# A two-stage attention kernel on one Trainium2 core: the exponentials of the window scores and the row maxima's copy, rest and parts are placed one step later in the written-out order of the steps

## What is computed

```
scores = einsum(q, k) / sqrt(16)
scores = exp(scores - max(scores))        # first exponential, row maximum over all 1024 keys
scores = where(-32 <= j - i <= 31, scores, 0)
weights = softmax(scores)                 # second exponential
x1 = layernorm(x + (weights @ v) @ Wo)
```

## Time and profile before

| what | value |
|---|---|
| median of 3 executions | 2041.89 us (2038.99 to 2049.73) |
| profiled execution, its own time | 2045.43 us |
| its span in the profile | 2043.6 us |
| TensorE busy | 1794.1 us (88%) |
| VectorE busy | 1602.4 us (78%) |
| ScalarE busy | 1342.1 us (66%) |
| GpSimd busy | 898.5 us (44%) |
| mean granted TensorE clock | 0.96 |

### The profile page before, as it was taken

One profiled execution on the slowest core, in us unless ns is written; L12 is line 12 of the kernel. 1 busy time (PEld: TensorE's weight loads), 2 busy tenths in 40 slices (PEclk: granted clock), 3 DMA queues, 4 the chain that ended last, 5 costly groups with the idle time before them and its releaser, 6 DMA issues. The chain is left out here.

```text
span 2043.6 us, 49487 instructions
## 1 busy us (share of the span) xinstructions
PE 1794.1 (88%) x16304; PEld 1334.9 (65%) x16304; DVE 1602.4 (78%) x4371; ACT 1342.1 (66%) x2643; POOL 898.5 (44%) x1338
## 2 busy tenths in 40 slices
PE   3989999999999999999999636878888699999997
PEld 2546556565565565565655526777787589999997
DVE  2788998988979979989889536978886477777775
ACT  2798898888888878888888315757664244344342
POOL 4323433566555645655565552000303755555411
PEclk8999999999999999999999658999998899999999
DMA  6443536446455464465354629888874333333211
GB/s 215 125 121 97 159 110 176 132 125 178 150 135 158 128 192 123 145 188 159 108 151 121 166 95 299 260 251 307 273 229 151 107 89 96 91 96 96 83 39 39
DMA packets 207317, 304.84 MB, mean 149 GB/s; under 512 B 48429, under 2 KB 108890, under 8 KB 207066
## 3 DMA queue, kind: packets, MB, share of 16 engines
q1 hardware_dynamic: 157322, 195.73, 32.7%
q0 software_dynamic: 29440, 68.98, 11.9%
q10 hardware_dynamic: 20304, 36.97, 4.9%
HBM read 104.16 MB, written 115.87 MB: 108 GB/s over the span
## 5 line engine op out<-in xcount | busy, mean ns | idle before, releaser
L1487 DVE CUSTOM_DVE_ANT_0 above<-p_half,above 128x512 f32<-128x512 f32 x1024 | 680.3, 684 | 102.0 <-ACT above L1171 79.7
L1171 ACT ACTIVATE above<-p_diff 128x512 f32<-128x512 f32 x1024 | 593.7, 600 | 88.8 <-PE p_diff L1047 85.7
L1047 PE MATMUL p_diff<-d_stack,q_stack 96*128 96x512 bf16 x1024 | 392.8, 386 | 30.2 <-ACT above L1171 15.7
L1051 PE MATMUL p_half<-k_stack,q_stack 96*128 96x512 bf16 x1024 | 388.7, 382 | 22.0 <-DVE row_max L1487 20.9
L1809 POOL DMA_INDIRECT raw<-sorted_y,slot x192 | 202.8, 1056 | 348.7 <-DMA sorted_y<-y_tile 293.6
L222 POOL DMA_INDIRECT sorted_x<-y,slot x192 | 198.6, 1035 | 95.9 <-issue 48.9
L2056 ACT ACTIVATE pt_hi<-p_one 128x512 fp32r<-128x512 f32 x128 | 69.5, 595 | 246.2 <-PE p_one L1932 246.2
L1192 ACT ACTIVATE w_win<-p_win 128x512 f32<-128x512 f32 x256 | 153.9, 601 | 50.1 <-PE p_win L1072 45.2
L1047 PEld LDWEIGHTS p_diff<-d_stack,q_stack 96*128 96x128 bf16 x1024 | 98.6, 98 | 110.9 <-ACT above L1171 49.3
L1051 PEld LDWEIGHTS p_half<-k_stack,q_stack 96*128 96x128 bf16 x1024 | 100.5, 99 | 96.6 <-DVE row_max L1487 78.3
L1200 ACT ACTIVATE w_win<-w_win 128x512 f32<-128x512 f32 x256 | 163.3, 638 | 0.2
(11 more groups left out here) (277 smaller groups left out, 4824.6 us busy)
## 6 DMA issues: line engine op xcount, KB each, us to landing
sorted_x<-zeros SPq DMA_DIRECT2D x141, 256.0 KB, 3.0
x_tile<-sorted_x SPq DMA_DIRECT2D x141, 256.0 KB, 4.1
sorted_y<-y_tile ACTq DMA_DIRECT2D x141, 256.0 KB, 3.6
q_stack<-q_parts SPq DMA_DIRECT2D x256, 96.0 KB, 2.4
k_stack<-k_parts SPq DMA_DIRECT2D x256, 96.0 KB, 2.4
d_stack<-d_parts SPq DMA_DIRECT2D x256, 48.0 KB, 2.0
v_win<-v_tiles POOLq DMA_DIRECT2D x16, 544.0 KB, 6.0
v_win<-v_tiles POOLq DMA_DIRECT2D x32, 272.0 KB, 6.8
```

The lines of the kernel that those rows point to most:

```text
L1047: nc.tensor.matmul(p_diff[s % 2][:], qs, d_stack[0:SPLIT_ROWS, h, :], start=True, stop=True).then_inc(s_diff, 1)
L1051: nc.tensor.matmul(p_half[s % 3][:], qs, k_stack[0:SPLIT_ROWS, h, HALO + S // 2:HALO + S], start=True, stop=True).then_inc(s_half, 1)
L1171: nc.scalar.activation(above[:, s % 4], p_diff[s % 2][:], ACT.Relu).then_inc(s_above, 1)
L1487: nc.vector.tensor_tensor_reduce(out=above[:, s % 4], in0=p_half[s % 3][:], in1=above[:, s % 4], scale=1.0, scalar=-3.0e38, op0=ALU.add, o ...
```

## The change

Two of the lags grow by one step. First and second exponentials of both halves go from 28, 31 and 29, 32 to 29, 32 and 30, 33. The maxima's copy on ScalarE and rest on VectorE go from one to two steps behind the transpose, and their parts and transfers on GpSimd from two to three. Nothing else moves; window scores stay at 27 and 30, and no wait is edited.

```diff
-EXP_LAGS, EXP2_LAGS = (28, 31), (29, 32)
+EXP_LAGS, EXP2_LAGS = (29, 32), (30, 33)
@@ GpSimd, unit
-                    for w, i, k in maxima(b, g, s, 2):
+                    for w, i, k in maxima(b, g, s, 3):
                         max_rows(w, i, k)
                     for j, kind, i in jobs(b, g, s, 3):
@@ ScalarE, unit
-                    for w, i, k in maxima(b, g, s, 1):
+                    for w, i, k in maxima(b, g, s, 2):
                         act.wait_ge(s_mt, k + 1)
                         wait(act, s_mrow, 48 * k)
                         nc.scalar.activation(m_parts[:, 0, :], p_max, ACT.Copy, scale=-1.0).then_inc(s_mhi, 1)
```

## The result

The kernel after takes 2139.8 us, the median of 6 runs (2134.6 to 2141.4), beside 2043.3 us of before in as many. The ratio is 1.0466, 95% interval 1.0446 to 1.0485: slower, by 95 us. The forecast was 2091, +49, with a range that ended at 2128. The direction was right, and the loss is nearly twice as large.

A forecast was written before the change was run, and what follows sets the result against it. TensorE, VectorE and ScalarE pass a wait around, none full. TensorE's delay of 54 us less the exponentials' 5 gives +49 on 2045.4, 2094.4, or 2091 us for the median; own range 2066 to 2115, 8-in-10 range 2060 to 2128.

The forecast's parts named there:

- The mechanism: TensorE's window scores wait for VectorE's `m_rest`, now behind max(S+2): L1064 starts at that maximum's start plus 1.0 us.
- event 1: Second of four places per unit where window scores wait for `m_rest`: L1064 2.0 us later, 1.0 us of it lost.
- The added wait of TensorE: Window scores held up by `m_rest`, summed over all places: 5.2 us for a unit, 84 us for 16.
- The exponentials' and the copies' own waits: On ScalarE: 45.2 us for window scores would become a wait for `p_diff`; the copies' 17.6 us for the transpose would go.
- step 1: Share of TensorE's added wait for `m_rest` that reaches the end: 6.7 us for a batch, 54 us for 8.
- the other events: First, third and fourth such waits per unit: 1.4 (g = 0) or 0.3 (g = 1), 0.2 and 1.3 us lost.
- step 2: Exponentials on ScalarE one step later: first ones gain 5 us (bounds nothing to 45.2), second ones cost nothing.
- step 3: Rival: longer TensorE gaps bring the 1.2 GHz clock into the steps, 225 us, about 2315 us; chance 0.03.
- Rival A: Every delay of TensorE reaches the end, with small bank waits on top: 2126, at most some 2135 us; chance 0.15.
- GpSimd's term: Parts and rows of the maxima one step later on GpSimd: cost nothing, up to 10 us if the cover went.
- the share of the second stage: The stage after the steps: as long as before, no added time.

The follow-up runs named there:

- run 3: Kernel after with four idle TensorE products put ahead of the waiting window scores at three of the four places per unit (all but the third): 1.0384 of before.
- run 1: Kernel before with the first and second exponentials alone one step later: 1.0094, +19 us.
- run 2: Kernel before with the maxima's copy, rest and parts alone one step later, exponentials as before: 1.0405, +83 us.
- E: Kernel before with the maxima's copy, rest and parts one step later at only some places: second of four per unit alone 1.0158, the other three 1.0228.
- F: Clock study: kernel after with four idle products ahead of late window scores, 1.0384; kernel before with only each unit's second place late, 1.0138 with such products, 1.0158 without.
- run 8: Kernel before with VectorE's rest of the maxima issued at the start of its step, ahead of the maximum: 1.0021 (0.9998 to 1.0043).
- run 5: Kernel before with the second exponentials alone one step later, first ones as before: 1.0056 (1.0025 to 1.0087), 11 us.
- run 9: Kernel before with GpSimd's parts and transfers of the maxima alone one step later: 1.0021 (1.0003 to 1.0038), 4 us.

## Why the prediction was wrong in size

The forecast was +49 us, and +95 came. Of the 46 us between them, 24 are the exponentials, some 17 the clock, and about 5 the wait and GpSimd's parts together.

**The mechanism** stood for the main part. L1064 waits for `m_rest`, which stands behind max(S+2). At event 1 it is 1.06 us from the start of that maximum to L1064 (526.92 to 527.98), where the prediction's terms give 1.2. From max(S+1) L1064 starts 2.86 us later instead of 0.99 (482.60 to 483.59), 1.9 us more, where it had 2.0. The added wait of TensorE was put at 84 us (its own terms add up to 82); the page shows 71. The exponentials' and the copies' own waits went as foretold, the latter to 0.2 us from the 17.6 of the earlier trace rows, and bought nothing.

**Failing step 1, what of the wait reaches the end: 54 us predicted, 59 to 66 measured** (run 3 less run 1, 1.0384 - 1.0094 = 59 us; run 2 less the clock's 17, 66 us), GpSimd's 4 us included and give or take 10. As a total this is the smallest of the misses and hardly clear of the noise; as a sum of terms it is not right. Event 1, "So 1.0 is lost", was put at 16 us and measured 28 to 32, and of the terms for the other events all but one were off, in ways that cancel (E). At event 1 the walk was right in kind, to the right instruction, and had the later pitch right (1.0 predicted, 0.98 to 1.00 in F). It erred in two places. It let the next Relu start 0.2 us after its `p_diff` and the maximum 0.6 after that; in F they start 0.42 and 0.76 us after (518.59, 519.01, 519.77), 0.4 later in all, of which 0.1 comes back because L1064 starts 1.06 us after max(S+2) instead of 1.2. And it stopped one maximum too soon: before, the fourth maximum followed the third by 0.61 us, now by 1.00. The 1.0 so becomes 1.25 at the third and 1.64 at the fourth, and the lower clock comes on top. The rule behind it, that a delay in a waiting engine is covered, holds at most while that engine has a reserve: the timeline shows 2 us using it up, and run 8, which was to show the cover for short waits, does not tell it from VectorE's own new wait.

**Failing step 2, the exponentials: -5 us predicted, +19 measured.** Two sentences were wrong. "Their reader, the weighted values at step 39, stands six steps behind. Nothing" looked only at who reads the second exponential, and not at who stands behind it in ScalarE's queue: the moved instruction falls into the step of the k copies, and 0.63 us of work then stands ahead of a Relu for which TensorE already waited (run 5, which moves the second exponentials alone, costs 11 us). And the possible gain was bounded below by nothing, when no row excluded a loss; the one loss that was priced, the later release of the bank, is not the one that came.

**Failing step 3, the clock: a rival of all or nothing, priced at 225 us with a chance of 0.03.** It came in part, about 17 us: the lower clock follows the longest waits, 1.8 us and more, and lasts 3.4 us each time instead of a head's 16 products at 64 places. The evidence against it was right for gaps of 0.67 us, and the prediction itself made gaps of 2.6 us there. Its one row at the lower clock, was also misread: the longest pause of TensorE in the 20 us ahead of it is 0.5 us, and from 1125.1 to 1127.9 it issues short products of 48 columns without a gap. The Trainium skill, "TensorE: Matmul & The Clock Gate", section "A second HAM failure mode: psum-queue depth-cycling", tells of one kernel whose frequent small idle gaps between groups of products made the clock swing. The traces here do not show that for small gaps (of 26 gaps of 0.5 to 1.5 us in before's steps one was followed by the lower clock) and do show it for the 25 gaps of 1.8 to 2.6 us in after, of which 20 were. That the clock was left out of the sum because the trace of before did not show it is the error: the change makes the condition that before lacks.

With 59, 19 and 17 the sum is 95 us, but it has to be: the 59 and the 17 are made from after, run 3 and run 1 by subtraction. What stands by itself is that the two parts of the change, 83 and 19, add up to 102 against 95, within their intervals. Rival A (all of the wait reaches the end, 2126 to 2135) lies nearer to 2140 than the forecast, by luck: not all of the wait reached the end, and the exponentials and the clock made up the rest. GpSimd's term, nothing, measured 4 us, and the share of the second stage, nothing, was right.

## What to carry to other kernels

- When a piece is moved by a step in an in-order queue, price it by what then stands behind it in each of the steps that it enters, and above all in the fullest one; how far its reader is matters only after that.
- A longer wait of one engine may be covered while the engine behind it still has work in store, and is felt once that is used up. Walk the pace-setter's starts on until the old and the new spacing agree for two instances, and take the difference there.
- If a change makes TensorE's gaps three times longer, the clock of the old trace is no evidence. Put in the sum what a stretch at the lower clock costs behind each long gap.

## What was not expected of the hardware

In the steps of after the granted clock was at 1.2 GHz in 21 stretches, most of them 3.4 us long. 20 of them follow the 25 idle gaps of TensorE of 1.8 to 2.6 us; of its 32 gaps of 0.5 to 1.4 us only one was followed by such a stretch. Four idle products at the end of such a gap were enough to keep the clock in most cases: 6 stretches are left (0.50 against 1.00 in the rows of F). And the same kernel before took 2143 us in one set of runs against 2045 in the others. The trace there with GpSimd's parts alone late (run 9) has 12 stretches at the lower clock, most of them at the end and in the first 11 steps of units; no trace of before itself was taken there, and what made that set slower is not known.
